# Moved GpSimd subtractions, a shorter end of a count search and a re-ordered projection in a two-layer attention and expert kernel

## The reference

```python
capacity = max(1, int(Sz * CAP_FACTOR / E) + 1)          # 1024 * 2 / 8 + 1 = 257
scores = softmax(einsum('bsd,ed->bse', x, router_w))
gate_vals, sel_idx = top_k(swapaxes(scores, 1, 2), capacity)
tokens = x[b_idx, sel_idx]
h = gelu(einsum('becd,edh->bech', tokens, w1) + b1)       # 128 -> 512
y = einsum('bech,ehd->becd', h, w2) + b2                   # 512 -> 128
out = zeros_like(x).at[b_idx, sel_idx].add(y * gate_vals)
```

## Time and profile before

| | us |
|---|---|
| runs, median of 3 | 973.85 (971.89 to 973.98) |
| profiled execution, its own time | 973.44 |
| its span, first to last instruction | 971.3 |
| TensorE busy | 841.9 (87%) |
| VectorE busy | 680.9 (70%) |
| ScalarE busy | 485.1 (50%) |
| GpSimd busy | 327.1 (34%) |

### The profile page before, as it was taken

The page is one execution under the profiler, slowest core; times in us unless marked ns, Lnnn a source line. Parts: engine busy times, 40 slices in busy tenths (PEclk is TensorE's granted clock), DMA queues, the critical chain, the costliest instruction groups (busy, mean ns, idle before and its releaser), DMA issues. The chain is left out here.

```text
span 971.3 us, 17219 instructions
## 1 busy us (share of the span) xinstructions
PE 841.9 (87%) x6170; PEld 544.3 (56%) x6170; DVE 680.9 (70%) x1750; ACT 485.1 (50%) x1044; POOL 327.1 (34%) x564
## 2 busy tenths in 40 slices
PE   5879999999998865899987889999999887589994
PEld 3545566655655533899964334444444435379993
DVE  7786676776773557988675867777777556698763
ACT  4325666666667430455424356666666664035450
POOL 2441134533321331255535112123322334035554
PEclk9998999999999979799979789999999998979996
DMA  4941131122001230024236360111000006002335
GB/s 98 269 126 29 34 83 42 26 66 62 23 18 29 82 93 5 2 24 69 25 61 163 86 175 2 34 34 34 1 2 2 2 1 175 1 6 21 47 45 109
DMA packets 58931, 53.55 MB, mean 55 GB/s; under 512 B 6672, under 2 KB 51872, under 8 KB 58464
## 3 DMA queue, kind: packets, MB, share of 16 engines
q1 hardware_dynamic: 44080, 43.37, 16.6%
q0 software_dynamic: 9216, 4.20, 4.9%
q10 hardware_dynamic: 5552, 4.89, 1.7%
HBM read 28.40 MB, written 22.94 MB: 53 GB/s over the span
## 5 line engine op out<-in xcount | busy, mean ns | idle before, releaser
L1006 ACT ACTIVATE b_pt<-b_banks 128x512 f32<-128x512 f32 (+1 forms) x320 | 154.8, 559 | 101.0 <-PE b_banks L920 100.8
L1029 DVE TENSOR_REDUCE a_mlate<-a_banks 128x2 f32<-128x1024 f32 (+3 forms) x120 | 124.8, 1079 | 51.0 <-PE a_banks L858 32.3
L1029 DVE TENSOR_REDUCE b_mlate<-b_banks 128x2 f32<-128x1024 f32 (+3 forms) x120 | 125.5, 1079 | 34.9 <-PE b_banks L868 17.5
L1273 POOL DMA_INDIRECT scratch_sum<-f_yg,f_index x64 | 100.0, 1563 | 102.7 <-DVE f_yg L1656 91.7
L920 PE MATMUL a_banks<-a_q,a_k 121*128 121x512 f32 (+3 forms) x384 | 117.3, 383 | 5.0 <-DMA a_q<-a_mt 4.0
L1006 ACT ACTIVATE a_q_hl<-a_banks 128x512 f32<-128x512 f32 (+1 forms) x160 | 81.8, 557 | 67.8 <-PE a_banks L920 66.3
L920 PE MATMUL b_banks<-b_q,b_k 64*128 64x512 f32 (+3 forms) x384 | 98.4, 417 | 12.7 <-ACT b_pt L1006 8.9
L1006 ACT ACTIVATE a_k_hl<-a_banks 128x512 f32<-128x512 f32 (+1 forms) x160 | 82.2, 557 | 53.6 <-PE a_banks L920 52.0
L858 PE MATMUL a_banks<-a_k,a_q 120*128 120x512 f32 (+3 forms) x384 | 99.1, 360 | 11.2 <-DVE a_mlate L1029 7.5
L920 PEld LDWEIGHTS b_banks<-b_q,b_k 64*128 64x128 f32 x384 | 47.2, 187 | 87.5 <-ACT b_pt L1006 55.5
L920 PEld LDWEIGHTS a_banks<-a_q,a_k 121*128 121x128 f32 x384 | 65.1, 190 | 50.3 <-issue 20.1
(11 more groups left out here) (243 smaller groups left out, 1453.3 us busy)
## 6 DMA issues: line engine op xcount, KB each, us to landing
scratch_sum<-zero SPq DMA_DIRECT2D x32, 128.0 KB, 2.1
f_raw<-in_w SPq DMA_DIRECT2D x16, 256.0 KB, 4.6
f_w<-in_w SPq DMA_DIRECT2D x16, 256.0 KB, 4.8
f_sums<-scratch_sum SPq DMA_DIRECT2D x8, 512.0 KB, 4.1
a_q<-scratch_q SPq DMA_DIRECT2D x8, 384.0 KB
a_k<-scratch_k SPq DMA_DIRECT2D x8, 384.0 KB
scratch_q<-b_q_hl SPq DMA_DIRECT2D x24, 128.0 KB, 2.8
b_q<-scratch_q SPq DMA_DIRECT2D x32, 96.0 KB
```

What stands on the lines that cost most here:

```text
L1006: act.activation(pt[at % NPT][:, h, 0:cols], st[u % NST][:, 0:cols], ACT.Exp, scale=scale).then_inc(exp_done, 1)
L1029: last = dve.tensor_reduce(dst, src, AX.X, ALU.max, negate=True)
L1273: pool.indirect_dma_start(sums_out[to], at(index[:, q, half:half + 1]), yg[q % NRING][:, half, :], None, compute_op=ALU.add).then_inc(scat ...
```

## The change

1. GpSimd in the experts: the first four `lower_matrix` wait until VectorE has normalised its last chunk. The other four and the last two `lower` no longer follow the search directly: one waits for the second set of `hots`, one for the first `gelu`, and the other four stand behind one of the first four scatters each.
2. ScalarE in the first layer's experts: four `split_matrix` stand ahead of the last `chunk_norm`.
3. ScalarE in both projections: the copy of the keys stands ahead of `chunk_norm`.
4. The fills of `vg` move from the first projection to the block of constants. `IDLE["attend"]` of the first layer goes from 34 to 6.
5. End of the search: two matmuls add into one accumulator column, and VectorE reads it there as a scalar; six instructions become three, and three become one.
6. Places count from 1 (the ruler `slot` too), which removes a subtraction of 1.

```diff
-                pool.iota(slot_i[:, :], [[1, COLS]], base=0, channel_multiplier=0).then_inc(counted, 1)
+                pool.iota(slot_i[:, :], [[1, COLS]], base=1, channel_multiplier=0).then_inc(counted, 1)
...
+                for t in m.vg:
+                    pool.memset(t[:, :, :, :], 0.0).then_inc(made, 1)
+                pool.wait_ge(made, 8)
+                for t in m.vg:
+                    pool.memset(t[:, :, :, HD:HD + 1], 1.0).then_inc(made, 1)
...
-IDLE = {"project": {"a": 0, "b": 0}, "attend": {"a": 34, "b": 10}, ...
+IDLE = {"project": {"a": 0, "b": 0}, "attend": {"a": 6, "b": 10}, ...
...
             act.activation(q_hl[:, 0, tok], q_ps, ACT.Copy).then_inc(first, 1)
+            act.wait_ge(mm, base + 2)
+            act.activation(k_dst(c, 0), k_src(), ACT.Copy).then_inc(first, 1)
             if c + 2 < NCH:
                 chunk_norm(act, m, s, c + 2, 4)
-            act.wait_ge(mm, base + 2)
-            act.activation(k_dst(c, 0), k_src(), ACT.Copy).then_inc(first, 1)
...
+        pool.wait_ge(norm.xn_by_vector, 3 * TPC)
         for e in range(NRING):
             lower_matrix(e)
         gate_parts()
-        pool.wait_ge(spotted, 1)
-        for e in range(NRING, NE):
-            lower_matrix(e)
-        for c in range(2, NCH):
-            lower(c)
         pool.wait_ge(m.sums_clear, 16 * 32)
+        pool.wait_ge(hot_ready, 2 * QT)
+        lower_matrix(NRING)
+        pool.wait_ge(gelu_done, HB)
+        lower_matrix(NRING + 1)
         for q in range(WORK):
             scatter(q)
+            if q < 2:
+                lower_matrix(NRING + 2 + q)
+            elif q < 4:
+                lower(q)
...
-            pe.matmul(c_ps[:, 0:1], m.peers[:, 0, :], count[:, 0:1], start=True, stop=True)
-            pe.matmul(c_ps[:, 1:2], m.peers[:, 1, :], count[:, 1:2], start=True, stop=True).then_inc(total_ready, 1)
+            pe.matmul(c_ps[:, 0:1], m.peers[:, 0, :], count[:, 0:1], start=True, stop=False)
+            pe.matmul(c_ps[:, 0:1], m.peers[:, 1, :], count[:, 1:2], start=False, stop=True).then_inc(total_ready, 1)
...
             take_x(0)
             take_x(1)
+            for e in range(NRING):
+                split_matrix(e)
             chunk_norm(act, m, norm, 2, 4)
...
+            link(dve.tensor_scalar(tied[:, :], tied[:, :], -FAR, FAR, ALU.mult, ALU.add))
             dve.wait_ge(total_ready, n_count)
-            link(dve.tensor_copy(totals[:, :], c_ps[:, 0:2]))
-            link(dve.tensor_tensor(need[:, :], totals[:, 0:1], totals[:, 1:2], ALU.add))
-            link(dve.tensor_scalar(need[:, :], need[:, :], -1.0, float(CAPACITY), ALU.mult, ALU.add))
-            link(dve.tensor_scalar(rank[:, :], rank[:, :], need[:, 0:1], None, ALU.is_le))
-            link(dve.tensor_tensor(tied[:, :], tied[:, :], rank[:, :], ALU.mult))
-            link(dve.tensor_tensor(take[:, :], above[:, :], tied[:, :], ALU.add))
+            link(dve.scalar_tensor_tensor(out=rank[:, :], in0=rank[:, :], scalar=c_ps[:, 0:1], in1=tied[:, :],
+                                          op0=ALU.add, op1=ALU.add))
+            link(dve.scalar_tensor_tensor(out=take[:, :], in0=rank[:, :], scalar=float(CAPACITY), in1=above[:, :],
+                                          op0=ALU.is_le, op1=ALU.add))
...
-            link(dve.tensor_copy(offset[:, :], c_ps[:, 2:3]))
-            link(dve.scalar_tensor_tensor(out=spot[:, :], in0=order_in[:, :], scalar=offset[:, 0:1], in1=take[:, :],
-                                          op0=ALU.add, op1=ALU.mult))
-            dve.tensor_scalar(spot[:, :], spot[:, :], -1.0, None, ALU.add).then_inc(spotted, 1)
+            dve.scalar_tensor_tensor(out=spot[:, :], in0=order_in[:, :], scalar=c_ps[:, 2:3], in1=take[:, :],
+                                     op0=ALU.add, op1=ALU.mult).then_inc(spotted, 1)
```

21 lines of the change are left out of this document (9 added, 12 removed).

## The result

The changed kernel took 979.47 us (median of 8 runs, 976.07 to 981.52) beside 974.45 for the kernel before: a ratio of 1.0049, 95% interval 1.0026 to 1.0073. It is slower, by half a percent; I had forecast 962. Four of all executions here lie far outside (the kernel before at 1827, 2452 and 4012 us, *a_in_flags* at 3606) and are not in the ratios. The profiled execution took 978.82 us (span 977.0, before 971.3).

What follows compares the result with a forecast made beforehand. TensorE, busy 87% of the span, was taken to bound the kernel, except where it waits or the chain runs through another engine. Terms -4.85 - 4.3 - 1.9 - 0.7 - 0.9 + 0.9 = -11.75 us gave 962 us, range 960 to 964.5.

Steps and rivals of the forecast that it cites:

- The failed step: Expert rounds: four subtractions behind scatters 1 to 4 cost nothing, VectorE waiting 1.14 us anyway and losing 1.0.
- My own bound: Expert rounds: if the cover of VectorE's wait were gone, the late subtractions would cost up to 4 us per layer.
- The hots' term: Experts, first hots to third pick: hots without subtractions beside them gain 4.85 us in layer 1, 4.3 in layer 2.
- The slower rival: Expert rounds: TensorE's hidden products and ninth pick wait for GpSimd's late subtractions, giving 976 us; chance 0.04.
- The end of the search: Experts, before the hots: fewer VectorE instructions gain 0.51 and 0.46 us, 0.97 per layer, 1.9 in all.
- The start of the first experts: Layer 1: softmax's last product freed of its subtraction gains 0.7 us; ScalarE's early weight copies cost 0 to 0.5.
- The first projection and attention: Opening: moved fills and 28 fewer fill-in matmuls gain 0.9 us, bounds -2.5 to +0.5.
- the next wait is the queue: Before the first score: only 0.9 of 4.6 us gets through, then ScalarE's queue issuing the maxima's DMA limits.
- The second projection: Second projection: ScalarE waiting for the key product ahead of the norm costs 0.9 us, between 0.3 and 1.4.
- The flags: Experts, second flags: held by subtractions as hots are, near 3.5 us; 1.6 if free.

Runs made afterwards that it cites:

- a_in_flags: Changed kernel with all six late GpSimd subtractions of a layer ahead of a scatter, each released by a round's first flag: 974.93 us, ratio to before 1.0022.
- dve_ahead: best_dve with each late subtraction on VectorE put ahead of a round's hots instead of behind its gates: 963.53 us, ratio to the kernel before 0.9903.
- a_gap: Changed kernel with all six late GpSimd subtractions of a layer ahead of a scatter, each released by a round's flags: 965.24 us, ratio to before 0.9920.
- b_pool: Kernel before with only the changed kernel's order of GpSimd's subtractions: 978.06 us, ratio 1.0056.
- best_dve: best with the six late subtractions of a layer done by VectorE between gates and sums: 961.14 us, ratio to the kernel before 0.9890.
- b_search: Kernel before with only the new end of the search and places counted from one: 968.69 us, ratio 0.9963.
- best: Kernel before with b_search's edits and a_gap's GpSimd order, opening and ScalarE's order as before: 965.36 us, ratio 0.9929.
- split_wait: Kernel before with only the early weight splits on ScalarE and GpSimd's first four subtractions behind VectorE's norms: 974.34 us, ratio 1.0007.
- a_rows_sp: Changed kernel with all four first rows of maxima on SyncE's queue, ahead of its two large loads: 974.08 us, ratio to before 1.0021.
- b_key: Kernel before with only the key copy ahead of ScalarE's norm, in both projections: 976.04 us, ratio 1.0029.
- a_key_back: Changed kernel with ScalarE's old order, norm ahead of key copy, in both projections: 975.69 us, ratio to before 1.0032.

## Why the prediction was wrong

**The failed step** is the one on the late subtractions: "The other four late subtractions lie behind scatters 1 to 4, in rounds in which VectorE waits 1.14 us for TensorE anyway and loses 1.0: I cost them at nothing." Both numbers of it were wrong. The 1.14 us is not slack for work that stands ahead of the hots: VectorE's gates release TensorE's index products, and VectorE waits for these; 0.68 us of the wait is that round trip (*dve_ahead*), 0.46 is slack. And the loss is 2.0, not 1.0, since the subtraction stands behind a scatter and VectorE is held from its issue on (*a_in_flags*). 1.6 us a round, in four rounds of each layer: +6.3 and +5.75 us where I had 0. Counted from the first scatter to the last, the layers grew from 78.67 to 85.43 us and from 78.75 to 85.37. Another place alone gave 13 us back (*a_gap*), 12.6 of them between these scatters (78.36 and 79.82), and the order alone made the kernel before slower by 0.56% (*b_pool*). My own bound, 4 us a layer if the cover were gone, did not reach it either, since it used the price of a subtraction behind another one.

**The hots' term** was right in mechanism and 1.45 and 1.6 us too large. VectorE did what was forecast: third hots 10.76 us after the first (forecast 10.5), second flags 3.78 (3.5). But I let TensorE be through its first products at about 11, without asking what TensorE waits for among them: it is these same second flags. It stood 2.13 us, ran on at 1.2 GHz, and ended the third pick at 15.07 instead of 13.6. The first layer of *b_pool* parts the two: the same stand of 2.13 us, no fall of the clock, third pick at 14.13. So the wait cost 0.5 us and the clock 0.9. With the flags free (*a_gap*) TensorE takes 0.28 us a product up to the third pick, which ends at 11.94. Nor is the third pick where a gain ends. The first scatter came 22.35 and 22.36 us after the first hots (before 26.19 and 25.96), and 21.35 and 21.24 in *best_dve*, where nothing is held: of 3.1 us at the pick 1.0 reach the scatters.

**The slower rival** was the wrong slower case. It had the right instructions and the wrong waiter: TensorE did not wait for the late parts; VectorE's next matrices, which had nothing to do with them, did.

**The end of the search** was right: 0.98 us (385.73 - 384.75) from the total's column to the scan for 1.55, three instructions for six, and 0.44 us less behind the count. But in the first layer only 0.13 of the 0.44 reached the hots: TensorE's four fill-in matmuls ahead of the turning of the places took 1.02 us at the lower clock (0.60 before), and VectorE waited 0.73 us for the turned places instead of 0.42. The same wait of 0.73 stands in the second layer of *b_search*, *a_gap* and *best*; fill-ins behind a chain that got shorter are a term that the prediction did not have. A scalar from the accumulator memory cost nothing (0.36 beside 0.35 us). The Trainium skill's 62 cycles more for a source there (VectorE: DVE Perf Modes, the section on the TRN2 errata) do not show for a scalar pointer in this trace.

**The start of the first experts** gave 0.77 us on the softmax's product as forecast, and lost it to the norm and what hangs on it: the weights' loads had not landed when ScalarE came for them (1.43 and 0.91 us of waits). I had read the DMA share of a window in which the splits did not yet ask for anything. Alone it lost 1.1 us in its stage (*split_wait*).

**The first projection and attention** came out at +1.65 instead of -0.9. The parts were near enough alone (-1.6 for fills and fill-ins, +1.4 for the key order); the step "the next wait is the queue" named the right queue, but not that one edit moves the maxima forward and the other the stores back, so that ScalarE's last row falls behind SyncE's loads; with all rows ahead of the loads the wait is gone (*a_rows_sp*).

**The second projection**: forecast +0.9, measured +1.0 (*b_key*), +1.6 (changed kernel) and -1.9 on taking it away (*a_key_back*), 1.3 between the means of all traces. Right in cause, near the upper end in size; the first chunk, for which I gave 0.1, waits 1.96 us for its keys.

**The flags** are held as hots are, as forecast. The Trainium skill's rule (SBUF — State Buffer, section "SBUF: two separate sides") has the port pair held for a whole instruction by whichever of the two engines started first, where VectorE runs a two-port mode. From it the prediction took that the late subtractions "would be held by hots in their turn". The trace agrees that one instruction carries the hold (the hot of 2.52 us), and shows the other direction: the hots are held by the subtraction, 2.0 us each time, although that hot's record starts 0.5 us ahead of the subtraction's.

## What to carry to other kernels

A wait of engine A for engine B is slack only for work that stands between A's last message to B and the wait; for everything ahead of that message only the part by which B itself is late counts as slack, and one instruction moved across the message measures it (5.96 us a round ahead of it, 5.69 behind). Work on GpSimd that shares VectorE's memory access is priced by where it falls in VectorE's round, not by how much of it there is: beside the gates five of the six subtractions had no price that shows and the sixth, in a round without a wait, stretched the hots by 1.05 us; in the flags each cost 0.8 to 0.9 us more than that, and behind a scatter 1.6. When an engine has free time next to such a gap and does the work in half the time (0.68 for 1.3 us), let it.

## What the runs showed of the hardware that I had not expected

- A GpSimd subtraction held VectorE from its issue on, even while GpSimd was still busy with a scatter: 1.58 us for 1.3 us of work with 0.34 us of scatter left, 2.0 with 0.55 left, 1.09 with none. Scatters alone did so little that hots took 2.3 us for 2.05.
- VectorE's gates, which read the accumulator memory and write SBUF, were not stretched by a subtraction beside them (0.60 us with and without).
- Four DMAs of 2 KB each held TensorE for 1.4 to 2.0 us where the last went out on another queue together with the first of two loads of 384 KB, and for 4.2 to 4.7 where it went out behind both; all four ahead of the loads on one queue held it for nothing, though one queue issues them more slowly (2.55 us for four).
- After TensorE had stood 1.9 to 2.2 us ahead of a round's products, some 3 us of the work that followed ran at the 1.2 GHz level in some layers (both of the changed kernel, the second of *a_gap*, *best* and *dve_ahead*) and at the 2.4 GHz level in others after the same stand (the first of *b_pool*, *a_gap* and *best*).
- The second attention, the same instructions in all kernels, took 274.05 to 279.95 us in single traces, at granted clocks of 0.98 to 0.94. No edit here explains the spread.
